# One score arena, smaller LayerNorm buffers, and two FFN chunks moved into the LayerNorm stage of a transformer layer on 8 cores

## What is computed

```python
x = x + _layernorm(attn(_layernorm(x), Wq, bq, Wk, bk, Wv, bv))
x = x + _layernorm(ffn(_layernorm(x), w_gate, w_up, w_down))
# attn: 16 heads of 64, blocks of 64 tokens; blocks 0 and 63 see all,
#       the others see block 0, their neighbours and block 63
# ffn:  h = silu(x @ wg.T) * (x @ wu.T);  h @ wd.T     (hidden 3072, int32 weights)
```

## Time and profile before

| | us |
|---|---|
| median of 2 runs | 2589.33 (2451.64 and 2727.03) |
| the profiled execution | 2449.68 |
| its span on the slowest core (core 2) | 2448.1 |
| spans of the 8 cores | 2425.8 to 2448.1 |
| start of `_p2`, of `_p3a`, of `_p4` within the span | 529.1, 971.2, 1339.9 |

### The profile page before, as it was taken

One profiled execution on the slowest core, in us unless ns is written; L12 is line 12 of the kernel. 1 busy time (PEld: TensorE's weight loads), 2 busy tenths in 40 slices (PEclk: granted clock), 3 DMA queues, 4 the chain that ended last, 5 costly groups with the idle time before them and its releaser, 6 DMA issues.

```text
span 2448.1 us, 31257 instructions; the slowest of 8 cores (2425.8 to 2448.1 us)
## 1 busy us (share of the span) xinstructions
PE 1655.7 (68%) x11110; PEld 801.8 (33%) x11234; DVE 849.1 (35%) x2276; ACT 602.5 (25%) x794; POOL 339.8 (14%) x511
## 2 busy tenths in 40 slices
PE   0059999937777773000000899999998999999994
PEld 0024444414444452000000344444443444444442
DVE  3414343322443345646664111222223232223123
ACT  2321111137666550112222101212111111112121
POOL 1011212101111122000000111111121212111210
PEclk9999999966766677555555899999999999999997
DMA  9943424351342224995553954566675866665752
GB/s 222 261 100 64 86 59 90 117 175 49 91 107 71 71 49 83 206 224 139 149 151 112 115 49 41 72 104 59 117 73 103 78 112 65 116 60 89 88 65 103
DMA packets 392665, 256.37 MB, mean 105 GB/s; under 512 B 345920, under 2 KB 347584, under 8 KB 390208
## 3 DMA queue, kind: packets, MB, share of 16 engines
q0 software_dynamic: 225728, 119.85, 33.7%
q1 hardware_dynamic: 152960, 100.95, 18.3%
q10 hardware_dynamic: 13824, 33.56, 4.0%
HBM read 214.05 MB, written 84.15 MB: 122 GB/s over the span
## 4 chain that ended last, share of the span: by engine, by line
PE 41%; DVE 7%; DMA 6%; SPq 3%; ACT 2%; issue 2%; ACTq 1%; DVEq 0%; POOL 0%; POOLq 0%
PE gp L941 14%; PE upp L947 14%; PE yp L959 7%; DMA xn_d<-p_xn 4%; PE upp L959 3%; PE gp L959 3%; SPq L680 2%; DMA p_ctx<-ctxT_d 2%; DVE p_x L756 1%; DVE y_sb L1021 1%; ACT p_xn L826 1%; DVE bst3b L762 1%; DVE bst3b L764 1%; DVE p_attn L718 1%; DVE p_attn L716 0%
## 5 line engine op out<-in xcount | busy, mean ns | idle before, releaser
L941 PE MATMUL gp<-x2T,wg_sb 128*128 128x512 bf16 x1504 | 373.1, 389 | 437.7 <-DMA x2T<-xn_d 400.1
L947 PE MATMUL upp<-x2T,wu_sl 128*128 128x512 bf16 x1507 | 364.9, 383 | 1.5
L941 PEld LDWEIGHTS gp<-x2T,wg_sb 128*128 128x128 bf16 x1536 | 152.2, 99 | 626.1 <-issue 452.4
L1009 DVE TENSOR_TENSOR hswb<-upp,sgbuf 128x512 bf16<-128x512 f32 x192 | 132.8, 692 | 588.0 <-PE upp L947 588.0
L887 POOL DMA_DIRECT2D wu_sl<-wuT x192 | 168.1, 878 | 991.0 <-PE upp L947 608.7
L580 ACT ACTIVATE aru<-psS 128x768 bf16<-128x768 f32 (+2 forms) x312 | 247.6, 849 | 124.3 <-PE psS L552 116.4
L986 ACT ACTIVATE sgbuf<-gp 128x512 bf16<-128x512 f32 x192 | 114.6, 597 | 573.7 <-PE gp L941 573.6
L552 PE MATMUL psS<-qt_buf,kt_buf 64*64 64x64 bf16 (+2 forms) x3232 | 165.2, 317 | 126.1 <-ACT aru L580 92.4
L947 PEld LDWEIGHTS upp<-x2T,wu_sl 128*128 128x128 bf16 x1536 | 152.0, 99 | 187.4 <-issue 10.8
L397 PE MATMUL qp<-xn1T,wq_sb 128*128 128x512 bf16 x490 | 121.5, 383 | 132.8 <-DMA xn1T<-xn_d 128.6
L959 PE MATMUL yp<-wd_sb,hswb 128*128 128x512 bf16 x752 | 194.9, 379 | 8.9 <-DVE hswb L1009 8.0
(11 more groups left out here) (85 smaller groups left out, 1214.5 us busy)
## 6 DMA issues: line engine op xcount, KB each, us to landing
wu_sl<-wuT POOLq DMA_DIRECT2D x192, 256.0 KB, 4.8
xbuf<-x_in SPq DMA_DIRECT2D x32, 512.0 KB, 11.1
p_x<-x_in SPq DMA_DIRECT2D x32, 512.0 KB, 9.9
x_d<-p_x ACTq DMA_DIRECT2D x32, 512.0 KB, 6.6
x1f<-x_d SPq DMA_DIRECT2D x32, 512.0 KB, 5.0
out<-obuf POOLq DMA_DIRECT2D x32, 512.0 KB, 5.7
v_d<-v_sb POOLq DMA_DIRECT2D x1, 8320.0 KB, 25.4
vu_buf<-v_d SPq DMA_DIRECT2D x8, 1040.0 KB, 11.0
```

What stands on the lines that cost most here:

```text
L941: mm = te.matmul(gsl, wg_sb[:, dc * FF + hc * 128:dc * FF + (hc + 1) * 128], x2T[:, par * 8 * 512 + dc * 512:par * 8 * 512 + (dc + 1) * 51 ...
L947: mm = te.matmul(usl, wu_sl[:, (hc % 4) * 1024 + dc * 128: (hc % 4) * 1024 + (dc + 1) * 128], x2T[:, par * 8 * 512 + dc * 512:par * 8 * 51 ...
L1009: v.tensor_tensor(hswb[:, hc * 512:(hc + 1) * 512], upp[:, (ghc % 2) * 512:(ghc % 2 + 1) * 512], sgbuf[:, (ghc % 2) * 512:(ghc % 2 + 1) * ...
```

## The change

- `v_sb` is kept in SBUF until the end of attention; `v_d`, its store and the loads of `vu_buf` are gone. In `_p1b` VectorE no longer waits for all stores of `_p1a` before it clears a column of `v_sb`.
- One arena `arenaB` in place of two, and one PSUM tensor `pp8` of 8 banks: scores have four buffers, and the context sums lie in the same banks. The order is scores(u), context(u), and scores(u+1) wait for VectorE's last copies of context(u).
- In `_p3a`, `p3_ctx` has 2 buffers in place of 8, `p3_x` 3 in place of 8, `p3_ln2` and `p3_xn2` 2 in place of 4.
- The FFN's gate/up of chunk 0, both down passes of chunk 0, and the gate/up of chunk 1 stand in `_p3a`'s TensorE program. ScalarE does six silus of chunk 0 behind its stage H in each of the iterations 6 to 9, and eight of chunk 1 in each of 13 to 15; VectorE does the multiplies behind its stage G in the same iterations, and two copies of outputs in iteration 11. The loads of `wd_sb` are placed between those of `wu_sl`.
- The down product is done in two passes of two tiles, which take turns in `yp`; `y_sb` has 2 tiles in place of 4, `x2T` 12 slots in place of 16, `wu_sl` 3 slices in place of 4. The silu goes into `hswb` and is multiplied there, in two halves.
- `_p4` starts with down(1, 0) and handles chunks 2 to 7, with the copy and the tail of an output tile one tile at a time.

The diff, cut to its core:

```diff
@@ helpers @@
+    def ffn_ycopy_t(v, gt):
+        pas = (gt % 4) // 2
+        v.wait_ge(sm.s_dph, 24 * (2 * (gt // 4) + pas + 1))
...
+    def ffn_gateup(te, c):
...
+            if ghc >= 2:
+                te.wait_ge(sm.s_hu, 2 * ghc - 2)
...
+    def ffn_down(te, c, pas):
+        te.wait_ge(sm.s_sg, 24 * (c + 1))
+        te.wait_ge(sm.s_hu, 48 * (c + 1))
+        te.wait_ge(sm.s_yraw, 4 * c + 2 * pas)
+        for hc in range(24):
+            te.wait_ge(s_wd_t[hc // 6], 16)
+            for k in (0, 1):
...
@@ _p1b, _p2 @@
-                g.wait_ge(sm.s_vev, 1 + V_COPY_TOTAL)
-                g.dma_start(v_d[:, :], v_sb[:]).then_inc(sm.s_vsp, 16)
...
-            nc.sbuf_tensor("aru0", [128, 2 * A], BF16) as aru0,
-            nc.sbuf_tensor("aru1", [128, 2 * A], BF16) as aru1,
-            nc.sbuf_tensor("vu_buf", [128, 2 * 32 * 130], BF16) as vu_buf,
+            nc.sbuf_tensor("arenaB", [128, 2 * A], BF16) as arenaB,
...
@@ _p3a @@
+            for it in range(6, 10):
+                sil_sched[it] = [(0, h) for h in range(6 * (it - 6), 6 * (it - 6) + 6)]
...
+            vec_sched[11] = [("y", 0), ("y", 1)]
+            for it in range(13, 16):
+                sil_sched[it] = [(1, h) for h in range(8 * (it - 13), 8 * (it - 13) + 8)]
...
-                    if t >= 8:
-                        sy.wait_ge(sm.s_v3a, t // 2 - 3)
-                        sy.wait_ge(sm.s_v4a, t // 2 - 3)
+                    if t >= 2:
+                        sy.wait_ge(sm.s_v3a, t // 2)
...
+                    if t >= 3:
+                        sy.wait_ge(sm.s_v4a, (t - 1) // 2)
+                    sy.dma_start(xb3[:, (t % 3) * DM:(t % 3 + 1) * DM],
...
+                    if t == 11:
+                        x2t_loads(sy, 0)
+                    elif t == 21:
+                        x2t_loads(sy, 1, dcs=[0, 1, 2, 3])
+                    elif t == 27:
+                        x2t_loads(sy, 1, dcs=[4, 5, 6, 7])
...
+                te.wait_ge(sm.s_wgu, 32)
+                ffn_gateup(te, 0)
+                ffn_down(te, 0, 0)
+                ffn_down(te, 0, 1)
+                ffn_gateup(te, 1)
...
+                    for (c, hc) in sil_sched.get(it, []):
+                        ffn_silu(s, c, hc)
@@ _p4 @@
+                ffn_down(te, 1, 0)
+                for c in range(2, NC4):
+                    ffn_down(te, c - 1, 1)
+                    ffn_gateup(te, c)
+                    ffn_down(te, c, 0)
+                ffn_down(te, NC4 - 1, 1)
...
+                tail_t(0)
+                tail_t(1)
+                for c in range(2, NC4):
+                    for g in range(4 * c - 6, 4 * c - 3):
+                        ffn_ycopy_t(v, g)
+                        tail_t(g)
+                    ffn_ycopy_t(v, 4 * c - 3)
+                    for hc in range(24):
+                        ffn_tt(v, c, hc)
+                    tail_t(4 * c - 3)
```

More of the change, by code:

```diff
@@ new lines, in ffn_down @@
+    def ffn_down(te, c, pas):
[5 more added lines that the diff above has]
+            for k in (0, 1):
+                tt = 2 * pas + k
+                for half in (0, 1):
+                    mm = te.matmul(
+                        hold["yp"][:, k * DM + half * 512:k * DM + half * 512 + 512],
+                        hold["hswb"][:, hc * 512 + tt * 128:
+                                      hc * 512 + tt * 128 + 128],
+                        hold["wd_sb"][:, hc * DM + half * 512:hc * DM + (half + 1) * 512],
+                        start=(hc == 0), stop=(hc == 23))
+            mm.then_inc(sm.s_dph, 1)
@@ new lines, in wu_loads, with x2t_gate @@
+    def wu_loads(g, c, hc0, hc1):
+        for hc in range(hc0, hc1):
+            ghc = 24 * c + hc
+            if ghc >= 3:
+                g.wait_ge(sm.s_gu, ghc - 2)
+            sl = hc % 3
+            g.dma_start(
+                hold["wu_sl"][:, sl * 1024:(sl + 1) * 1024].rearrange(
+                    "p (dc e) -> p dc e", dc=8),
+                wuT_d[:, hc * 128:(hc + 1) * 128].rearrange(
+                    "(dc p) e -> p dc e", p=128)).then_inc(s_wu_t[sl], 16)
+    def x2t_gate(c, dc):
+        s = (8 * c + dc) % 12
+        for cc in (c - 1, c - 2):
+            if cc >= 0 and (s - 8 * cc) % 12 < 8:
+                return 24 * (cc + 1)
+        return 0
@@ new lines, in x2t_loads @@
+    def x2t_loads(sy, c, dcs=None):
+        if dcs is None:
+            dcs = sorted(range(8), key=lambda d: x2t_gate(c, d))
+        sy.wait_ge(sm.s_sp3b0, 64 * (c + 1))
+        sy.wait_ge(sm.s_sp3b1, 64 * (c + 1))
+        gcur = 0
+        for dc in dcs:
+            gq = x2t_gate(c, dc)
+            if gq > gcur:
+                sy.wait_ge(sm.s_gu, gq)
+                gcur = gq
+            slot = (8 * c + dc) % 12
+            sy.dma_start_transpose(
+                hold["x2T"][:, slot * 512:(slot + 1) * 512],
+                xn2_d[c * 512:(c + 1) * 512, dc * 128:(dc + 1) * 128]).then_inc(
+                (sm.s_x2t0, sm.s_x2t1)[c % 2], 16)
@@ L475, in _ @@
             def _(sy):
[L476 to L495, removed]
@@ L530, in _ @@
+                        ctxb[:, (t % 2) * 1040:(t % 2 + 1) * 1040],
+                        ctxT_d[:, t * 128:(t + 1) * 128]).then_inc(s_ct[t % 2], 16)
             @blk.tensor
             def _(te):
[L532 to L554, removed]
-                                            kt_buf[rows:rows + 64,
-                                                   up + j * 64: up + j * 64 + 64],
-                                            rhs, start=True, stop=True,
-                                            tile_position=(rows, tcol))
-                                col += w
-                            last.then_inc(sm.s_spe, 1)
-                    if u >= 1:
-                        ctx_emit(te, u - 1)
@@ L993, in _ @@
+                ln4_t(0)
+                ln4_t(1)
+                for c in range(2, NC4):
+                    for g in range(4 * c - 6, 4 * c - 3):
+                        ln4_t(g)
+                    for hc in range(24):
+                        ffn_silu(s, c, hc)
+                    ln4_t(4 * c - 3)
+                for g in range(26, 32):
+                    ln4_t(g)
             @blk.vector
```

496 lines of the change are left out of this document (253 added, 243 removed).

## The result

The changed kernel takes 2610.79 us (median of 9 runs), the kernel before 2453.22 (median of 8). The ratio is 1.065, its 95% interval 1.063 to 1.067: slower by 6.5%. The forecast was 2622.

What follows compares the result with a forecast made beforehand. TensorE's 400.1 us wait through the LayerNorm stage was the largest. The stage starts at 944; plus 656 gives 1600, plus FFN 1020 gives 2620, plus 1.6 around the span gives 2622 us; range 2510 to 2790.

Steps and rivals of the forecast that it cites:

- V's round trip: Before attention: without V's store and its barrier, scores begin about 1 us after 502.5 instead of 529.11, saving 25.6 us.
- One arena: Attention: a round goes from 50.9 to 53.4 us, but an idle stretch at the end falls away; -2 us, ±15.
- The LayerNorm stage: LayerNorm stage: grows from 369 to 656 us, through loads between iterations, slow weight loading and FFN slices.
- The step from A to E's statistics: LayerNorm iteration: A to E takes 12.3 us and E until its statistics 5.6, the iteration's own 17.9.
- 9 together: LayerNorm cycle: four issues and a landing of 3.1 to 6.2 us take 9 us, in a cycle of 27.
- The iterations with slices: LayerNorm stage: iterations 6 to 9 take 43.2 us each, iteration 13 takes 60, iterations 14 and 15 take 50 each.
- The FFN: FFN block: shrinks from 1108 to 1020 us; a chunk takes 153.1, with copy waits of 16 and 8.5.
- the forecast case: Whole kernel: the main forecast of 2622 us, said to go from 2555 to 2715; chance 0.60.
- Rival 3: LayerNorm stage: down-weight quarters meet transposes, each taking 23.4 us to issue; about 75 us more, 2697 us; chance 0.10.
- that the stage absorbs the work: LayerNorm stage: FFN multiplies fit into waits, stage 369 + 36 us; total time 2371 us, faster by 3.2%; chance 0.10.
- That TensorE stays at the low clock through its bursts: LayerNorm stage: a slice takes 6.9 us in place of 3.45, 108 us more, total time 2730 us; chance 0.12.
- The rival of fast loads: LayerNorm stage: loads land fast, cycle stays 20.7 us, weights delay little; 100 us less, total time 2522 us; chance 0.08.

Runs made afterwards that it cites:

- the version with both orders: Changed kernel with SyncE's p_ctx transposes ahead of the waiting x load and VectorE's copies side by side ahead of FFN multiplies: 2343.05 us, ratio 0.958.
- the kernel with VectorE's order mended: Changed kernel with two output tiles' copies together on VectorE, those of down(c-1, 1) ahead of chunk c's multiplies: 2447.63 us, ratio 1.001.
- the kernel with only the slices spread: Changed kernel with FFN slices spread between LayerNorm stages: two behind A and B, two behind E and F, the rest behind G and H: 2591.74 us.

## Why the prediction was right

The time came out 11 us under the forecast, within its range, by the forecast's own mechanism. By its steps:

- **V's round trip, -25.6.** Right: the wait shrank by 26.7, and the store put back costs 21. The first scores come 33.7 us earlier on the slowest cores (28.6 by the mean over all eight). Of the rest, 5.5 are there at the first projection already, which starts at 142.4 in place of 147.9; the dropped wait at the head of `_p1b` was not tested by itself.
- **One arena, -2, with bounds of ±15.** Wrong in size, outside its bounds: the block is 25.6 shorter on the slowest cores, and 27.5 by the mean over all eight (440.7 to 413.2). The step that failed is "ScalarE's exponentials fill 32.1 of it without gaps, so four score buffers in place of two bring nothing". The row had no gap between instructions, and yet they could follow each other faster. With two buffers those of 1024 columns are 0.90 us apart (8.12 / 9) and those of 768 are 0.79 (23.76 / 30); with four the mean over all is 0.744 (29.03 / 39). The rest of that sum was right: with two buffers the one-arena round is 53.7, forecast 53.4.
- **The LayerNorm stage, 656.** Measured 677.6. A(1) came at 50.9, not 60: the transpose took 22.00 to issue, as expected, but landed sooner. From there to A(6) it took 161.6 in place of 148, since most plain cycles are 32 and not 27.2. The step from A to E's statistics is right (17.9); the term "9 together" for issues and landing was mis-sized, it is 4.6 + 9.1. It lay within the stated bounds of 24 to 33. The iterations with slices hold: 44.0, 45.0, 44.4 and 46.4 for 43.2; 62.9 for 60; 51.6 for 50.
- **The FFN, 1020.** Measured 1014.6: the start 20.8 after the barrier for 27.4, two passes and a wait 53.3 for 54.3, six chunks of 153.6 for 153.1, the end 19.2 for 19. The two waits are 15.77 and 8.44 for 16 and 8.5.

So attention's miss (-32 at the start of the stage, some 8 of it the earlier barrier), the stage's (+22) and the FFN's (-5) partly cancel. The sum is better than its parts, and that much of it is luck.

Two figures beside the sum don't follow from their own terms. The upper end of the forecast case, "2715", is 2622 + 60 + 15 = 2697 by what stands in its brackets. Rival 3's "about 75" would be 92 with two transposes of 23.4 in each of three iterations less 16 covered in each. Neither touches the forecast.

The rivals: that the stage absorbs the work is false for the changed kernel, where iterations with slices take 44 to 63 us, and for the version with both orders, where they take 43 to 61 in place of 18. That TensorE stays at the low clock through its bursts is false, as TensorE's timeline of after shows:

```profile
1150.83 3.57 PE L237 MATMUL gp<-x2T,wg_sb 128*128 128x512 bf16 x8 [23.18 <-DVE hswb L207]
1154.19 3.01 PE L242 MATMUL upp<-x2T,wu_sl 128*128 128x512 bf16 x8
1157.04 1.89 PE L237 MATMUL gp<-x2T,wg_sb 128*128 128x512 bf16 x7
```

Two groups take 3.36 and 2.85 us from start to start, and the third is at 1.73 again: after 23 us of waiting the recovery takes 6.2 us, about what the earlier trace rows showed after 5. The Trainium skill, "TensorE: Matmul & The Clock Gate", section "HAM oscillation — how this bites in real kernels", says that bursts between waits start cold each time. The trace agrees for waits of 8.44 us and more (passes of 22.5 to 23.6 in place of 20.88); for waits of 2.78 us it is mixed, as the kernel with VectorE's order mended showed. The rival of down-weight quarters that meet the transposes is false in the changed kernel: from iteration 6 on no transpose of `p_ctx` takes over 3.4 us to issue. Its mechanism is real all the same, as the kernel with only the slices spread shows, where one takes 18.46. The rival of fast loads is false in the changed kernel, whose cycle is 32.

## What to carry to other kernels

In a queue that works in order, the wait of one load is the wait of all behind it: issue first what has the earliest free buffer. When one engine both frees a buffer and does other work, put the copy that the other engine waits for ahead of all that can come later; here two reorderings of existing instructions were worth 116 and 163 us, and together they turned a loss of 6.5% into a gain of 4.2%. And before work is moved into an idle stretch of one engine, count what it takes on the engines that aren't idle there: 215 us of FFN moved into 400 us of TensorE's idle time gained 21 at most.

## What was not expected of the hardware

- **Score buffers.** A stretch of ScalarE without idle time in the profile need not be at its best rate: the same 39 exponentials took 32.3 us with two PSUM buffers and 29.03 with four, in one kernel with one number changed. A single one of 768 columns is not shorter with four, it is longer (1.10 us in place of 0.81), but the next one starts before it ends; with two buffers they hardly overlap. First two buffers, then four (count, then busy us and mean ns of one):

```profile
L667 ACT ACTIVATE arenaB<-pp 128x768 bf16<-128x768 f32 x232 | 176.1, 808 | 11.9 <-PE pp L624 2.3 <-issue 0.3
```
```profile
L667 ACT ACTIVATE arenaB<-pp 128x768 bf16<-128x768 f32 x232 | 164.8, 1098 | 0.0
```

  What hinders the overlap with two is not shown.
- **Loading eight tiles ahead was not faster.** In the kernel before, stage E waited for stores in ten iterations (61.0 us in all), in cycles of 20.7 us. In the version with both orders and no FFN in the stage, with two and three buffers, E waits for a store once, and cycles are 18.3. The pages of the two, on the x loads (KB each, then median us to landing), first before:

```profile
p_x<-x_in SPq DMA_DIRECT2D x32, 512.0 KB, 9.9
```
```profile
p_x<-x_in SPq DMA_DIRECT2D x32, 512.0 KB, 5.0
```

The whole stage takes 369 and 375 us, although A(1) and A(2) come 53 and 90 us after A(0) in the second and 9 and 27 in the first. The weights, issued at the same point in both, delay the kernel before only later (A(4) and A(5) come 33 and 41 us after the one ahead), and its cycles behind them are longer. Stores land more slowly there too: those of `xn_d` in 9.2 us (median, from 1100 to 1300 us) in place of 5.4 (from 1080 to 1240). The order of SyncE's queue differs as well as the number of buffers, so which of them makes the later cycles shorter is not shown.
